# Binarised 3x3 convolution with group norm: the work of its weight stage is divided and ordered anew, and its first tile is begun early

## The reference

```python
def bconv(x, M, Z, alpha, rv):          # M (256,256,3,3), Z (8,256,256,3,3), rv (1,8)
    A = m*m + sum_k(z_k*z_k) / 100
    w = m/sqrt(A) + sum_k rv_k * z_k/sqrt(A)
    bw = sign(w)                        # binary weights
    ba = sign(x)                        # binary activations
    return conv3x3(ba, bw, padding=1) * alpha
out = x + bconv(group_norm(x, 32 groups), M, Z, alpha, rv)      # x (64,256,28,28) f32
```

## Time and profile before

| | |
|---|---|
| median of three runs | 524.27 us (523.59 to 525.61) |
| the profiled execution | 522.31 us |
| its span in the trace | 520.5 us |
| TensorE busy with matmul | 482.7 us (93%) |
| VectorE busy | 375.4 us (72%) |
| ScalarE busy | 328.8 us (63%) |
| first product of the convolution | 81.01 us |

### The profile page before, as it was taken

How to read it: one execution, slowest core, us unless ns; L and a number is a source line. 1 busy time by engine, 2 the same in 40 slices (tenths; PEclk the granted TensorE clock), 3 DMA queues, 4 the chain that set the end, 5 groups by cost and what they waited for, 6 DMA issues and landing times.

```text
span 520.5 us, 8289 instructions
## 1 busy us (share of the span) xinstructions
PE 482.7 (93%) x2794; PEld 401.2 (77%) x2794; DVE 375.4 (72%) x711; ACT 328.8 (63%) x566; POOL 22.8 (4%) x70
## 2 busy tenths in 40 slices
PE   0898969899999999999999999999999999999990
PEld 0454637788888888888888888888888888888880
DVE  1122458757977978878879879879779779776656
ACT  0787766577667667676676676676676766754320
POOL 8200000000000000000000000000000000000000
PEclk9999997989999999999999999999999999999996
DMA  6999958018568578568568568568577577544226
GB/s 235 399 396 396 397 216 345 0 63 309 214 220 307 191 243 276 211 243 290 191 242 287 195 241 295 191 241 292 197 251 273 210 261 268 202 148 186 87 100 247
DMA packets 45644, 124.37 MB, mean 239 GB/s; under 512 B 3632, under 2 KB 3632, under 8 KB 45616
## 3 DMA queue, kind: packets, MB, share of 16 engines
q1 hardware_dynamic: 45616, 124.01, 65.8%
HBM read 72.62 MB, written 51.38 MB: 238 GB/s over the span
## 4 chain that ended last, share of the span: by engine, by line
PE 86%; DVE 4%; DMA 3%; ACT 2%; SPq 2%; issue 2%; DVEq 0%; ACTq 0%
PE conv_ps L353 80%; DMA m_sb<-in_L_conv_M_dram 3%; SPq L245 2%; PE conv_ps L294 2%; ACT whole L409 1%; DVE x_sb L699 1%; PE conv_ps L307 1%; DVE bn L623 1%; PE conv_ps L297 1%; PE conv_ps L311 1%; PE grp_ps L337 1%; DVE low L605 0%; ACT signs L459 0%; DVE whole L673 0%; ACT low L414 0%
## 5 line engine op out<-in xcount | busy, mean ns | idle before, releaser
L353 PE MATMUL conv_ps<-signs,wts 128*128 128x492 f32 (+5 forms) x1926 | 425.5, 381 | 2.4 <-ACT signs L459 2.1
L353 PEld LDWEIGHTS conv_ps<-signs,wts 128*128 128x128 f32 x1926 | 361.6, 190 | 59.0 <-ACT signs L459 2.5
L467 ACT ACTIVATE part<-conv_ps 128x492 int32<-128x492 f32 (+3 forms) x107 | 61.4, 574 | 147.0 <-PE conv_ps L353 147.0
L459 ACT ACTIVATE signs<-x_sb,shift,rstd 128x784 fp32r<-128x784 f32 x128 | 125.8, 1035 | 0.8 <-DVE shift L660 0.8
L673 DVE SCALAR_TENSOR_TENSOR whole<-conv_ps,part 128x492 int32<-128x492 f32 (+3 forms) x107 | 70.9, 663 | 73.5 <-PE conv_ps L353 65.2
L681 DVE SCALAR_TENSOR_TENSOR low<-whole,conv_ps 128x492 f32<-128x492 int16 (+3 forms) x107 | 70.5, 659 | 3.7
L699 DVE SCALAR_TENSOR_TENSOR x_sb<-whole,alpha_sb,x_sb 128x784 f32<-128x784 int16 x64 | 66.0, 1031 | 0.7
L699 DVE SCALAR_TENSOR_TENSOR x_sb<-low,alpha_sb,x_sb 128x784 f32<-128x784 f32 x64 | 65.9, 1029 | 0.0
L642 DVE BATCH_NORM_STATS2 bn<-x_sb 128x6 f32<-128x392 f32 x116 | 59.7, 557 | 0.8 <-issue 0.6
L437 ACT ACTIVATE unread<-x_sb 128x784 bf16<-128x784 f32 x58 | 49.2, 848 | 0.0
L439 ACT ACTIVATE unread<-x_sb 128x784 bf16<-128x784 f32 x58 | 49.1, 847 | 0.0
(11 more groups left out here) (46 smaller groups left out, 150.5 us busy)
## 6 DMA issues: line engine op xcount, KB each, us to landing
x_sb<-in_x_dram SPq DMA_DIRECT2D x64, 784.0 KB, 5.7
out_dram<-x_sb SPq DMA_DIRECT2D x64, 784.0 KB, 3.8
x_sb<-in_L_conv_Z_dram SPq DMA_DIRECT2D x64, 288.0 KB, 7.4
m_sb<-in_L_conv_M_dram SPq DMA_DIRECT2D x8, 288.0 KB, 8.3
alpha_sb<-in_L_conv_alpha_dram SPq DMA_DIRECT2D x2, 0.5 KB, 2.4
rv_sb<-in_L_conv_rv_dram SPq DMA_DIRECT2D x1, 4.0 KB, 2.4
```

The lines of the kernel that those rows point to most:

```text
L353: mm = pe.matmul(sums_of_tile(b, skip, drop), wts[:, ch, kh * KW + kw], e, start=n == 0, stop=n == PRODUCTS - 1, skip_group_check=True)
L459: nc.scalar.activation(o, x_sb[:, slot_of(t, j), h].rearrange("p (a b) -> p a b", b=W), ACT.Sign, bias=shift[:, t % BODY, j, h:h + 1], sca ...
L467: nc.scalar.activation(part[:, bank(b), 0:columns(b)], conv_ps[bank(b)][:, 0:columns(b)], ACT.Copy, scale=-FRACTION / PACK, bias=FRACTION ...
```

## The change

- A quarter of the squares (two of the eight draws) goes from ScalarE to VectorE. M squared is no longer added by TensorE: VectorE adds it to the sum of the others (`unit_a_sum`) and writes the result to SBUF, from where ScalarE takes the root. `m_sq` has four buffers in place of two.
- In each turn ScalarE does the root and the sign of the older units first and then the squares of the new one; VectorE does w first, then its squares, then `unit_a_sum` of the unit before.
- Image 0 is loaded behind load 3 in place of load 4. The last load comes in two parts, one for each unit (18 DMAs of half the columns).
- The first half of the taps is packed in turns 11, 12 and 13, one round in each, and copied in turns 12 to 14. Of the second half, all three rounds are copied by ScalarE; its last round has a third bank.
- Sums A and q have changed banks, so that tile 0's bank is free once unit 14 is done. The nine products of tile 0 that need only the first half of the channels run before the second half is packed. All tiles wait for the two halves of an image's signs one after the other.
- Image 0's statistics are spread over turns 9 and 10; its group follows in turn 11, its signs in turn 13 (first half) and behind the last sign of the weights (second half).
- Images 1 and 2 go through the group norm one by one. The second triple's group is done behind tile 2 in place of tile 3, its first image's signs behind tile 3. VectorE takes images 1 to 5's statistics in small portions between the other steps.

```diff
 SQ = 2
+MQ = 4
...
-        q_ps = conv_ps[0:3]
-        a_ps = conv_ps[3:5]
-        taps_ps = wt_ps
+        a_ps = conv_ps[0:2]
+        q_ps = conv_ps[2:5]
+        taps_ps = [wt_ps[0], wt_ps[1], wt_ps[0], wt_ps[1], wt_ps[0], a_ps[1]]
...
+                parts = 1 if c < LOADS - 1 else 2
+                for u in range(parts):
...
-                if c == LOADS - 4:
+                if c == LOADS - 5:
                     load(0, 0, 0, True)
...
             def unit_a(c):
                 pe.wait_ge(z_squares_done, c + 1)
-                need(pe, inv_done, c - 1)
+                pe.wait_ge(dve_squares_done, c + 1)
+                need(pe, a_full, c - 1)
...
-                pe.wait_ge(m_squares_done, c + 1)
-                for j in range(KQ):
-                    mm = pe.matmul(a_ps[c % 2][...], one[...], m_sq[:, c % SQ], start=False, stop=True)
...
             unit_a(UNITS - 1)
-            pack_taps(1)
-            group(1, 0, 1, TRI, TRI)
+            pe.wait_ge(signs_done, 1)
+            pe.wait_ge(act_wts_done, 2)
+            pe.wait_ge(dve_wts_done, 1)
+            pe.wait_ge(a_full, UNITS - 1)
+            products(0, 0, 0, TAPS)
+            pe.wait_ge(a_full, UNITS)
+            for n in range(TAP_ROUNDS, HALVES * TAP_ROUNDS):
+                pack_taps(n)
+            group(1, 0, 1, 2, 2)
+            pe.wait_ge(act_wts_done, HALVES * TAP_ROUNDS - 1)
...
+                        if first and t == 0 and b == 0:
+                            group(2, 0, 2, TRI, TRI)
...
-                nc.scalar.activation(z_sq[:, c % SQ], z, ACT.Square).then_inc(z_squares_done, 1)
+                nc.scalar.activation(z_sq[:, c % SQ, 0:ACT_DRAWS], z, ACT.Square).then_inc(z_squares_done, 1)
...
             for c in range(UNITS):                      # ScalarE
-                unit_squares(c)
                 if c >= INV_LAG:
                     unit_inv(c - INV_LAG)
                 if c >= SIGN_LAG:
                     unit_sign(c - SIGN_LAG)
+                unit_squares(c)
...
             unit_sign(UNITS - 1)
-            copy_taps(4)
-            copy_group(1, 0, 1, TRI)
-            deviation(1, 0, 1, TRI)
+            half_signs(0, 0, 0, 0, 1)
+            for n in range(TAP_ROUNDS, HALVES * TAP_ROUNDS):
+                copy_taps(n)
+            copy_group(1, 0, 1, 2)
+            deviation(1, 0, 1, 2)
             image_signs(0, 1, 0, 1)
+            copy_group(2, 0, 2, TRI)
...
+                nc.vector.tensor_tensor(z_sq[:, c % SQ, ACT_DRAWS:K], z, z, ALU.mult).then_inc(dve_squares_done, 1)
...
+            def unit_a_sum(c):
+                dve.wait_ge(a_done, c + 1)
+                dve.wait_ge(m_squares_done, c + 1)
+                nc.vector.tensor_tensor(m_sq[:, c % MQ], a_ps[c % 2][:, 0:CW], m_sq[:, c % MQ],
+                                        ALU.add).then_inc(a_full, 1)
...
             for c in range(UNITS):                      # VectorE
-                unit_m_squares(c)
                 if c >= INV_LAG:
                     unit_w(c - INV_LAG)
+                unit_m_squares(c)
+                if c >= 1:
+                    unit_a_sum(c - 1)
...
+            unit_w(UNITS - 2)
+            stats_of_both(1, 0, 1)
+            unit_a_sum(UNITS - 1)
+            stats_of_both(1, 1, 2)
+            unit_w(UNITS - 1)
+            stats_of_both(1, 2, 4)
+            sums_of_both(1)
+            stats_of_both(2, 0, 2)
+            bounded(1, 0, 1, 2)
+            stats_of_both(2, 2, 3)
+            negative_mean(1, 0, 1, 2)
+            stats_of_both(2, 3, 4)
+            sums_of_both(2)
+            stats_of_both(3, 0, 4)
+            sums_of_both(3)
+            bounded(2, 0, 2, TRI)
...
```

More of the change, by code:

```diff
@@ L73, in conv_preact @@
     QUAD = 32
+    ROW_ORDER = (1, 0, 2)
     KQ = P // QUAD
@@ L388, in body @@
                         number = k * TILES + b
-                        first_products(k, t, b, min(b + 1, TRI), number)
-                        if b == (3 if first and t == 0 else 0) and width(t + 1, last) > 0:
-                            group(k + 2, t + 1, 0, width(t + 1, last), k * TRI + TRI + width(t + 1, last))
+                        first_products(k, t, b, min(b + 1, TRI), number, TAPS if first and t == 0 and b == 0 else 0)
+                        if first and t == 0 and b == 0:
+                            group(2, 0, 2, TRI, TRI)
+                        if b == (2 if first and t == 0 else 0) and width(t + 1, last) > 0:
+                            group(k + 3, t + 1, 0, width(t + 1, last), k * TRI + TRI + width(t + 1, last))
                         if not (first and t == 0 and b == 0):
@@ L509, in body @@
                         fraction(b, k * TILES + b)
[L510 to L513 removed]
+                        if b == (2 if start else 0):
+                            copy_group(k + 3, t + 1, 0, then)
+                        if b == (3 if start else 1):
+                            deviation(k + 3, t + 1, 0, then)
+                        if start and b == 3:
+                            image_signs(k + 1, k + 3, t + 1, 0)
                         if not start and 2 <= b < 2 + then:
[L515 removed]
+                            image_signs(k + 1, k + 3, t + 1, b - 2)
                     if start:
[L517 to L518 removed]
+                        for j in range(1, TRI):
+                            image_signs(k + 1, k + 3, t + 1, j)
             bodies(act, body)
@@ L569, in _ @@
             variance(0, 0, 0, 1)
-            variance(1, 0, 1, TRI)
+            variance(1, 0, 1, 2)
+            variance(2, 0, 2, TRI)
             def body(r, count, first, last):
@@ L574, in body @@
                     if width(t + 1, last) > 0:
-                        variance(r * BODY + t + 2, t + 1, 0, width(t + 1, last))
+                        variance(r * BODY + t + 3, t + 1, 0, width(t + 1, last))
             bodies(pool, body)
@@ L741, in body @@
                             outputs(t - 1, b - 1, end)
-                        if b == (3 if start else 1):
-                            bounded(k + 2, t + 1, 0, then)
-                        if b == (4 if start else 2):
-                            negative_mean(k + 2, t + 1, 0, then)
+                        if not start and b == 1:
+                            bounded(k + 3, t + 1, 0, then)
+                        if b == (3 if start else 2):
+                            negative_mean(k + 3, t + 1, 0, then)
                         if start and b == 2:
                             sums(r, t + STAT_LEAD, 0, lambda: None)
+                            bounded(k + 3, t + 1, 0, then)
             bodies(dve, body)
```

163 lines of the change are left out of this document (87 added, 76 removed).

## The result

The changed kernel takes **511.76 us** in the median (511.06 to 512.73, four runs), the kernel before, run beside it, 524.37. The ratio is 0.976, 95% interval 0.974 to 0.979. The forecast was 512.3 from 524.27, a gain of 12.0; the first measurement gives 12.6.

What follows compares the result with a forecast made beforehand. TensorE, gapless from 110 us, bounds the kernel, so its full-speed start sets the end: 105.4 less 92.75 is 12.6 us, less 0.6 for low clock gives 12.0, from 524.27 to 512.3 us; range 508.0 to 517.5.

Steps and rivals of the forecast that it cites:

- packing: Start of packing the second half of the taps, replayed at 71.3 us, 5.2 before the 76.51 of before.
- product 87: Early convolution, first product after the old wait for image 3's signs; replayed at 92.75 us, with 0.6 for low clock.
- The bound, right.: Convolution: from 110 to 510 us TensorE is busy 398.6 of 400 us, and the change doesn't touch it.
- The chain replayed: Each engine's instructions in new order from load 5 (49.13 us) into the first tiles; 12.6 us gained before low clock.
- the 0.6 held back for it: Weight stage: net loss to low clock after TensorE's 3.9 us gap, 0.3 to 1.3 us, taken as 0.6.
- The landing of the last load: End of weight stage: load in two parts takes 7.9 us, unit 15 there at 62.6 to 63.7, not binding.
- the three signs that the prediction named for being wrong: Packing later than 74, TensorE wait over 2 us after it, or a wait for load 7's last part.
- last load late: Weight stage: DMA pieces cost by number, so the load takes 13.4 us; gain 7.1, time 517.2 us; chance 0.07.
- The stall before product 87: TensorE's 2.08 us wait for image 3's signs and its low clock (1.71 us lost) would be gone.
- The low clock: Weight stage: after a 3.9 us gap, 1.2 GHz costs units 8 and 9 up to 2 us, most given back.
- The rival with a spell at the handover: Low clock after gaps of 1.5 or 1.4 us at the handover; costs 1.7, 514 to 516 us; chance 0.2.
- the 105.4: Kernel before: full-speed start of product 87, 103.66 us plus 1.71 lost to low clock.

Runs made afterwards that it cites:

- second trace: The changed kernel run once more with no edit, against the kernel before: 512.90 us, ratio 0.979, span 510.5.
- The three runs that take it away: Changed kernel with the last load in one part (512.20 us), with image 0 behind load 4 again (511.78), and with both edits (511.98).

## Why the prediction was right, step by step

| step | predicted | first trace | second trace |
|---|---|---|---|
| gap of TensorE before unit 8, us | 3.9 | 3.59 | 3.91 |
| load 6 there (q of 12 starts) | 55.85 | 56.31 | 56.21 |
| squares, ScalarE and VectorE, us | 1.62, 0.76 | 1.63, 0.75 | 1.63, 0.75 |
| q of unit 15 | 64.3, behind w of 12 | 66.92, behind the load | 65.23, no wait |
| packing | 71.3 | 73.43 | 72.41 |
| wait before group 2, us | 1.4 | 1.16 | 1.16 |
| wait before tile 2, us | 0.45 | 0.29 | none |
| from packing to product 87, us | 21.45 | 22.1 | 23.0, with a spell |
| product 87 | 92.75 and 0.6 | 95.5 | 95.4 |

**The bound, right.** The convolution from 110 us on is as before (388.6 busy of 390 us), and the span moved by what product 87 moved, in both pairs of traces, to 0.1 us: from there to the end it is 415.1 to 415.2 us in all four.

**The chain replayed, right in its pieces, 1 to 2 us short in its sum.** ScalarE's pieces from unit 12's squares on follow each other as replayed: 15.1 us from these squares to the packing by the prediction (56.2 to 71.3), 15.5 measured in the second trace. Of the 1.1 us by which that trace's packing is late, 0.7 was there at unit 12. Load 6 came 0.36 later than reckoned, and a spell lies in units 8 and 9 (43.6 to 47.1, and 43.8 to 47.3 in the first trace). With image 0 behind load 4 and no spell there, the squares of unit 12 start 0.3 us earlier (56.62 for 56.92), so the spell with its gap cost about half of the 0.6 held back for it. The first trace is 1.0 later still, by the last load. Two prices were a little off besides. The 0.2145 us of a product is a mean with the short matmuls of `group` in it; products alone are 0.218 apart (90 in 19.66 us from 98.55), 0.3 us in the 77 from the handover to product 87. And the two rates that give 17 ns a piece give 15, and 7.7 us for the load.

**The landing of the last load, the term that was mis-sized.** The prediction let the first part go "at 48 to 49.5" and the last leave at "60.4 to 62, just in time", and concluded that "neither landing time binds". The wait ended at 50.06, the last DMA was issued from 61.76 to 62.35, and the engines, fed at 230 and then 201 GB/s, had no backlog. I had priced pieces (7.9 us a load) and issues (12.4 us) each by itself and not asked which of the two sets the rate once the backlog is gone. And the time from the last issue to its landing, which the prediction put at some 2 us (60.4 to 62 for the one, 62.6 to 63.7 for the other), was 5.1 us in one trace and 3.5 in the other; with the last issue in nearly the same place (61.76 and 61.45) this is most of what put the load on the path in one and not in the other. A wait for the last part of load 7 is one of the three signs that the prediction named for being wrong, and the first trace has it, 1.47 us. The rival "last load late" named a cost by number of pieces; that isn't it, since the same DMAs with a backlog were moved at 353 to 379 GB/s, near the priced 336. What there is is a cost by number of issues, and the landing of the last. It was worth 1.0 us in one trace and not 4.9. The three runs that take it away are 0.7 to 1.1 us shorter than the changed kernel in their series and no shorter than its first four runs.

**The stall before product 87, right**, cause and cure: image 3's signs are 2.5 us ahead of need, and the group norm moved back brings a wait of 1.23 us.

**The low clock, half right.** That a gap of nearly 4 us in the weight stage would be followed by 1.2 GHz was right in both traces, but not in every run: gaps of 3.75 us (before unit 8, in the run without early products) and 3.64 (before unit 10, with image 0 behind load 4) had no spell behind them. The rival with a spell at the handover, given 0.2, is in the second trace (77.8 to 81.2), behind a wait of 1.16 us, shorter than the 1.91 that I took for harmless.

**The total.** The two pairs of traces hold 9.9 and 11.5 us, the medians 12.6 and 11.1, against 12.0. The first median lies within 0.6 of the forecast partly by luck: the stage went 1 to 2 us worse than replayed, and the kernel before has in its median a later place of product 87 than the profiled execution from which I took the 105.4. Its second trace shows such a run: loads and packing 0.9 us later, and more of the same spell under products.

**Where it came from.** In the first traces 3.1 us lie before the packing (76.51 to 73.43) and 6.8 between it and product 87 (28.9 to 22.1, the low clock behind product 87 counted). For the latter the rows give 2.07 for the stall, 1.71 for its spell, 1.4 for the part of the spell from 77.0 to 83.9 that lies under products (2.85 us), 1.9 for the nine products and 2.05 for the packing, from its start to the first product behind it (4.50 us before, 76.51 to 81.01; 2.45 after, 73.43 to 75.88). That is 9.2 in all, less the 1.45 of the two new waits behind it: 7.7, where 6.8 were measured. Some of the rest is that a wait costs more than its row says: from 75.88 five products at 0.218 us are over at 76.97, and TensorE goes on at 78.41, 1.44 us later, where the row has 1.16. The low clock in the old packing itself cost nothing: it takes 4.50 us in both traces, though the spell begins 0.5 us into it in one and 1.7 in the other.

Undone one at a time, order, squares, place of the group norm and early products each cost 0 to 2.2 us. That they replace each other in part, or save a spell that doesn't come in every run, would explain it and isn't shown. Not undone by themselves, and so not separated, are M squared off TensorE, image 0's signs in two halves, the taps packed a round a turn, the shorter packing (copies on ScalarE alone, a third bank), and images 1 and 2 one by one.

## What to carry to other kernels

Replay the few instructions of each engine across a stage boundary with durations from rows, and take the place from which the bound engine runs without a gap as the one number; it gave the span to 0.1 us in both pairs. When a load is cut into more DMAs, compare the issuing engine's rate with what the DMA engines move, from the moment when the backlog is used up, and add the time from the last issue to its landing. And take two traces of each kernel before a difference of 2 us between them is explained: here spells of low clock and landing times moved by as much between runs of one program.

## What the runs showed of the hardware that was not expected

- The same wait is followed by low clock in one run and not in another. The 2.07 us gap before product 87: low clock in both traces of the kernel before (1.71 us lost each), none in that with the new order. A gap before unit 4 had none behind it in the first trace of the changed kernel (2.88 us), but with image 0 behind load 4 (2.58 us) there is a spell from 27.0 to 30.4. Gaps of 3.59 and 3.91 us before unit 8 had a spell behind them, one of 3.75 there had not. The wait of 1.16 us before group 2 had one behind it in the changed kernel's second trace and in none of the eight other traces that have this wait.
- SyncE's issues stand 0.64 to 0.75 us apart whether each moves 288 or 144 KB. Nine of 144 KB that leave 0.64 us apart, with no backlog, are 230 GB/s, and the DMA engines are then busy for 0.81 to 0.91 of the time; with a backlog DMAs of 144 KB were moved at 353 to 379 GB/s and those of 288 KB at 397.
- From the issue of the last 144 KB DMA to its landing it was 5.1 us in one trace of the changed kernel and 3.5 in the other.
